# Edge lists on another queue, longer filling turns, and two normalisations tile by tile in a two-layer graph kernel

## The reference

```
xn = layernorm(x)
x  = x + relu(sum_i w[i] * (adj/degree)^i @ (xn @ W + b)) + gamma_norm(linear_attention(xn))
x  = x + top2_experts_16(layernorm(x))
xn = layernorm(x)
x  = x + gat(xn, edges) + linear_attention(xn) @ W_out + b_out
x  = x + top2_experts_8(layernorm(x))
```

## Time and profile before

| | |
|---|---|
| median of three runs | 230.09 us (229.31, 230.09, 230.31) |
| the profiled execution's own time | 230.77 us |
| its span | 229.1 us |
| mean granted TensorE clock | 0.968 |
| TensorE busy with matmuls | 215.6 us, 94% |
| VectorE busy | 138.9 us, 61% |
| ScalarE busy | 63.6 us, 28% |
| GpSimd busy | 21.2 us, 9% |
| chain that ended last | PE 88%, DVE 6%, DMA 2%, the rest 4% |

### The profile page before, as it was taken

How to read it: one execution, slowest core, us unless ns; L and a number is a source line. 1 busy time by engine, 2 the same in 40 slices (tenths; PEclk the granted TensorE clock), 3 DMA queues, 4 the chain that set the end, 5 groups by cost and what they waited for, 6 DMA issues and landing times.

```text
span 229.1 us, 2847 instructions
## 1 busy us (share of the span) xinstructions
PE 215.6 (94%) x989; PEld 142.1 (62%) x989; DVE 138.9 (61%) x414; ACT 63.6 (28%) x148; POOL 21.2 (9%) x36
## 2 busy tenths in 40 slices
PE   7399999998999799999999999999979999899994
PEld 4288455675589579854556686478754544758741
DVE  2799989958599442340636449797934764834202
ACT  2512755333220121110010149730643302013100
POOL 3680010000010200000050000000300010200000
PEclk9859999999999799999999999999999999999979
DMA  4899897599350000046040000000000000000002
GB/s 137 313 383 363 264 417 306 190 363 417 132 183 1 3 0 0 0 152 217 26 157 0 3 0 1 0 0 3 0 0 0 0 3 0 0 1 3 0 0 92
DMA packets 8669, 23.65 MB, mean 103 GB/s; under 512 B 2376, under 2 KB 2376, under 8 KB 8400
## 3 DMA queue, kind: packets, MB, share of 16 engines
q1 hardware_dynamic: 8656, 23.48, 28.3%
HBM read 22.95 MB, written 0.52 MB: 103 GB/s over the span
## 4 chain that ended last, share of the span: by engine, by line
PE 88%; DVE 6%; DMA 2%; issue 1%; POOL 1%; SPq 1%; ACT 0%; DVEq 0%
PE bank L1158 17%; PE bank L1132 13%; PE bank L1262 10%; PE bank L1250 10%; PE bank L1169 7%; PE bank L1207 6%; PE bank L1314 3%; PE bank L1213 3%; PE bank L1146 2%; PE bank L1214 2%; PE bank L1198 2%; DMA xa<-in_x 2%; DVE xT L604 2%; PE bank L1301 1%; PE bank L1351 1%
## 5 line engine op out<-in xcount | busy, mean ns | idle before, releaser
L1158 PE MATMUL bank<-raw,xT 128*128 128x512 f32 x88 | 39.2, 594 | 0.0
L1158 PEld LDWEIGHTS bank<-raw,xT 128*128 128x128 f32 x88 | 16.2, 190 | 18.3 <-issue 18.2
L309 POOL TENSOR_TENSOR rstd<-veps,minus_half 128x1 f32<-128x1 f32 x14 | 8.7, 632 | 163.0 <-DVE veps L591 89.0
L1262 PE MATMUL bank<-raw,ring 128*128 128x512 f32 x48 | 22.7, 634 | 0.0
L1250 PE MATMUL bank<-xT,raw 128*128 128x256 f32 x96 | 22.7, 386 | 0.0
L798 DVE TENSOR_SCALAR ring<-iota_bf,edges,radix 128x128 bf16<-128x128 bf16 x64 | 20.3, 359 | 0.0
L1250 PEld LDWEIGHTS bank<-xT,raw 128*128 128x128 f32 x96 | 17.6, 190 | 3.1 <-issue 0.9
L1301 PE MATMUL bank<-iota_bf 128*128 128x256 bf16 x121 | 17.6, 306 | 1.9 <-DVE iota_bf L775 1.6
L1169 PE MATMUL bank<-xT,raw 128*128 128x256 f32 x64 | 17.4, 434 | 0.8 <-DVE xT L604 0.8
L1262 PEld LDWEIGHTS bank<-raw,ring 128*128 128x128 f32 x48 | 9.6, 202 | 12.1 <-issue 11.7
L1301 PEld LDWEIGHTS bank<-iota_bf 128*128 128x128 bf16 x121 | 12.9, 108 | 5.8 <-DVE iota_bf L775 1.6
(11 more groups left out here) (256 smaller groups left out, 333.8 us busy)
## 6 DMA issues: line engine op xcount, KB each, us to landing
raw<-in_up SPq DMA_DIRECT2D x6, 512.0 KB, 8.6
raw<-in_down SPq DMA_DIRECT2D x6, 512.0 KB, 10.7
raw<-in_k SPq DMA_DIRECT2D x4, 512.0 KB, 9.7
raw<-in_q SPq DMA_DIRECT2D x4, 512.0 KB, 11.3
raw<-in_v SPq DMA_DIRECT2D x4, 512.0 KB, 9.8
raw<-in_out SPq DMA_DIRECT2D x4, 512.0 KB, 6.5
raw<-in_gat SPq DMA_DIRECT2D x4, 512.0 KB, 6.8
raw<-in_gnn SPq DMA_DIRECT2D x2, 512.0 KB, 10.7
```

The lines of the kernel that those rows point to most:

```text
L1158: ins = mm(bank[banks[t]][:, :], xT_at(c, t), w.at(c), start=c == 0, stop=c == C - 1)
L1262: ins = mm(dst, hid[:, m, cols], w.at(m), start=m == 0 and not opened, stop=m == k - 1)
```

## The change

Four edits:

- The two edge lists are issued by ScalarE, as the first two instructions of its block, and no longer by SyncE ahead of x.
- TensorE's idle turns before the first transposes are 30, not 20, and six more stand between those transposes and k0.
- In layer 0 the attention residual of a tile is complete in one piece (`mixture`): tile 0 ahead of diffusion step 0, tile 1 ahead of step 1. The third step's add, the residual, the statistics and the normalising pass run tile by tile (`residual`). TensorE transposes tile 0, runs the eight turns, and transposes tile 1.
- Before the last feed-forward the `elu`, the statistics and the normalising pass run tile by tile (`last_elu`). TensorE runs four turns, transposes tile 0, runs 24 turns, and transposes tile 1.

```diff
         def _(sp):
-            for a, n in enumerate(("src", "dst")):
-                sp.dma_start(edges_i[:, a, :], A[n].rearrange("(p j) -> p j", p=P)).then_inc(edges_in, 16)
             for t in range(T):
...
+            for a, n in enumerate(("src", "dst")):
+                nc.scalar.dma_start(edges_i[:, a, :], A[n].rearrange("(p j) -> p j", p=P)).then_inc(edges_in, 16)
             act.wait_ge(iota_bf_ready, 1)
             act.wait_ge(turn_ready, 1)
...
-            diffuse(0)
-
-            def centred(t):
+            def mixture(t):
+                dve.wait_ge(o_full, t + 1)
+                variance(1, t, bank[t][:, :])
                 go(V.scalar_tensor_tensor(mixed[:, t, :], bank[t][:, :], mv[:, t, 0:1], row["gamma0"],
                                           ALU.subtract, ALU.mult))
-
-            for t in range(T):
-                dve.wait_ge(o_full, t + 1)
-                variance(1, t, bank[t][:, :])
-                if t == 0:
-                    centred(0)
-            dve.wait_ge(step_read, 2)
-            diffuse(1)
-
-            centred(1)
-            settle()
-            for t in range(T):
+                settle()
                 dve.wait_ge(rstd_ready, T + t + 1)
                 V.scalar_tensor_tensor(mixed[:, t, :], mixed[:, t, :], rstd[:, t:t + 1], xa[:, t, :],
                                        ALU.mult, ALU.add).then_inc(mix_ready, 1)
+
+            mixture(0)
+            diffuse(0)
+            mixture(1)
+            dve.wait_ge(step_read, 2)
+            diffuse(1)
             dve.wait_ge(step_read, 4)
             dve.wait_ge(mix_ready, 2)
 
-            for t in range(T):
-                add_step(2, t)
-            for t in range(T):
+            def residual(t):
                 dve.wait_ge(step_read, 4 + t + 1)
                 go(V.scalar_tensor_tensor(xb[:, t, :], diffused[:, t, :], 0.0, mixed[:, t, :], ALU.max, ALU.add))
-            variances(2, lambda t: xb[:, t, :])
+                settle()
+                variance(2, t, xb[:, t, :])
+
+            add_step(2, 0)
+            residual(0)
+            add_step(2, 1)
             dve.wait_ge(xT_full, 2)
-            for t in range(T):
-                norm_rows(2, xn[:, t, :], xb[:, t, :], t)
+            norm_rows(2, xn[:, 0, :], xb[:, 0, :], 0)
+            residual(1)
+            norm_rows(2, xn[:, 1, :], xb[:, 1, :], 1)
...
-            elu(1, xb, summed, mixed, go)
-            variances(6, lambda t: xb[:, t, :])
-            for t in range(T):
+            def last_elu(t):
+                dve.wait_ge(y_ready, T + t + 1)
+                go(V.scalar_tensor_tensor(mixed[:, t, :], g_a[:, t, :], 0.0, summed(t), ALU.max, ALU.add))
+                settle()
+                dve.wait_ge(elu_exp, T + t + 1)
+                go(V.scalar_tensor_tensor(xb[:, t, :], g_b[:, t, :], 1.0, mixed[:, t, :], ALU.min, ALU.add))
+                settle()
+                variance(6, t, xb[:, t, :])
+
+            for t in range(T):
+                last_elu(t)
                 norm_rows(6, xn[:, t, :], xb[:, t, :], t)
...
-            idle_turns(1, 20)
+            idle_turns(1, 30)
             pe.wait_ge(consts, 1)
             xT_made(0, xn, (0, 1))
+            idle_turns(2, 6)
             k_of("k0", k_full, 0)
...
+            xT_made(1, xn, (4, 5), (0,))
             idle_turns(5, 8)
-            xT_made(1, xn, (4, 5))
+            xT_made(1, xn, (4, 5), (1,))
...
-            idle_turns(4, 40)
-            xT_made(4, xn, (3, 4))
+            idle_turns(4, 4)
+            xT_made(4, xn, (3, 4), (0,))
+            idle_turns(4, 24)
+            xT_made(4, xn, (3, 4), (1,))
```

## The result

The changed kernel took 233.60 us (median of four runs, 232.48 to 233.77) beside 229.70 us of the kernel before (229.15 to 230.31): ratio 1.0173 [1.0129, 1.0217] (in brackets the 95% interval), slower, where 226.5 was predicted. Both deny the prediction. Both kernels spread over almost 5 us from run to run, and the changed one's time goes with its mean granted clock: 228.5 to 228.9 at 0.975 to 0.977, 230.2 to 230.6 at 0.968 or 0.969, 233.4 and 233.5 at 0.953 and 0.955. The first four runs all lay at the dear end (233.61 at 0.956 in the profiled one), where only four of the twelve later ones lie; whether four in a row were chance stays open.

The account below looks back on a forecast made before the run. The prediction took TensorE's own time and the few places where it waits as the bound. Terms -3.0 + 0.7 - 1.6 = -3.9 gave 226.9 or 226.2, stated as 226.5 us; range 225.6 to 227.5, widened to 224.6 to 229.0.

Parts of the forecast that it names:

- Part 1, -3.0: Start: x issued earlier and more idle turns keep the clock up beside k0; last counts end near 38.55, -3.0 us.
- 6.9 predicted: Start: k0's records at the upper clock level take 6.9 us, not 9.93.
- 0.8 or less: Start: TensorE idles 0.8 us or less before the normalised rows come, instead of 2.70.
- the one-hots are late next: Start: first counts wait for VectorE's one-hots and end at 19.6 instead of 23.00, a gain of 3.4 us.
- The 0.8 for an earlier x: Start: x, issued 0.91 us earlier, lands 0.8 us sooner.
- I had allowed them 0.6 us: Start: edges landing up to 0.6 us later still hide behind an x that lands at 4.9.
- Rival 4: Start: late edges delay the statistics; total +2.9, 233.4 us; slower once edges land after 5.8; chance 0.04.
- Part 2, +0.7: Middle of layer 0: TensorE waits 0.7 us for low parts before the third diffusion step; +0.7 us.
- nothing is gained and the 0.7 stays: Middle of layer 0: VectorE is ready for both halves in time, TensorE's work stays the same; the 0.7 us wait remains.
- rival 3: Middle of layer 0: the clock falls earlier, while narrow records still run; term +2.3, total 228.1 us; chance 0.14.
- The rule that I set against this row: Middle of layer 0: clock follows recent busyness, so no fall behind 5 us of unbroken work; sum 1.6 us lower.
- Part 3, -1.6: Before the last feed-forward: tile 0's work runs in VectorE's wait, tile 1 ends at 198.35 instead of 199.98; -1.6 us.

Follow-up runs that it names:

- the larger comparison: The changed kernel repeated without an edit (12 runs) beside more runs of the kernel before (30), on one chip: 230.33 against 230.55 us, ratio 0.9988.
- the part alone: Kernel before with only the start changed: edges on ScalarE's queue, 30 and 6 idle turns; 230.95 us, ratio 1.0011.
- part 2 alone: Kernel before with only the middle of layer 0 changed, in VectorE's order and TensorE's turns; 231.58 us, ratio 1.0088.
- the wide products: Narrow attention-weight products made 128 columns wide by repeating columns; on the changed kernel 226.41 us, with the middle of layer 0 in the old order 226.22.
- the change without part 2: Changed kernel with the middle of layer 0 as before, start and last feed-forward edits kept; 228.91 us, ratio 0.9822.
- the kernel with the lowest median: Kernel before with products 128 columns wide, the tile-by-tile last feed-forward, and 30 and 6 idle turns, edges still on SyncE; 224.03 us, ratio 0.9777.

## Why the prediction was wrong

**Part 1, -3.0: half right, and read from one unlucky start.** The kinds held: k0 at a granted clock of 1.00 takes 7.14 us (6.9 predicted), though TensorE stood for 1.68 us before the transposes and not for 0.8 or less, the one-hots are late next (TensorE's loads wait for VectorE's ring at 20.05), and the last counts end 2.1 us earlier. Two sizes failed. The 0.8 for an earlier x was 0.36 (5.84 to 5.48), because the statistics now wait for the edges, converted at 4.62 instead of 3.37. I had allowed them 0.6 us; they took 1.25. Rival 4 named this wait, with its point of decision at a landing of 5.8, which they did not reach. And the profiled start of before was no typical one: x was late there (5.84) and k0 took 9.93. In four other traces with the edges and x issued as before, x is there at 5.05 to 5.20; in one, at 6.07. Out0 then begins at 53.59 to 53.70 with the old turns, against 54.85 in the profiled execution of before. With part 1 it begins at 52.58 to 52.91. So the part is worth about 0.9 us there, not 3.0, and by the part alone (1.0011) even that is lost further on. In the larger comparison this term is the furthest off.

**Part 2, +0.7: the step that failed in the first comparison.** The forecast of the wait was right, in place and nearly in size (0.47 us before the third step, forecast 0.7), and VectorE had both tiles ready (71.15 and 74.10) before TensorE asked. What failed is "nothing is gained and the 0.7 stays", that is, a clock that falls only behind the narrow records. In the first profile the part took 6.6 us: from 2.1 early to 4.5 late. Of these 0.5 are the wait, 1.1 the diffusion step (65.69 to 68.83 for 2.08), 4.8 the narrow records, 0.3 the rest. That is rival 3's mechanism, priced there at "as much again" as 1.7; a whole narrow stretch at half rate costs 4.8. I had its price in the rows: 48 records at twice 0.11 us. Over ten runs part 2 alone costs 1.1 us by the medians and 2.0 by the ratio, and with the wide products no cost shows. So the price is that of the clock and not of the order, as far as these runs tell: the fall came at 66.5 and 71.3 us in two traces of the same kernel, and kernels without part 2 have low stretches of up to 14 us as well.

The rule that I set against this row says that the clock follows how busy the engine has been (the Trainium skill, TensorE: Matmul & The Clock Gate, What's actually happening). If busy is what the profile shows as busy, the traces disagree for narrow records: TensorE ran without a gap from 65.69 to 78.88, and the granted clock was 0.50 from 67 on. The same section of the Trainium skill says that what watches the activity runs free of the kernel's start, so that the moment of the change behind the first matmuls shifts by half a microsecond either way. The traces agree that changes shift from run to run, and for this fall, in the middle of a kernel, by more: 66.5 and 71.3 us in the same kernel, whose 48 records took 10.05 and 6.62 us.

**Part 3, -1.6: right.** The delay shrinks from 4.5 to 2.8 us between layer 0 and the router, so -1.7; tile 1 is normalised by 202.81, 3.9 us after out1's end at 198.9 (forecast 3.8). Alone it gave 0.9909, -2.1 us (-1.2 by the medians of all runs).

**The sum.** Forecast were -3.0, +0.7 and -1.6; the parts alone gave +0.3, +2.0 and -2.1 by the ratios, and the whole -0.3 [-1.3, +0.8]. Two steps failed: that the clock of the middle falls only behind the narrow records, which cost 6.6 us in the first trace, and that the start of one trace is the kernel's, which made -3.0 out of -0.9. Two of the signs named for being wrong came: the statistics waited for the edges, and the middle lost more than 1 us. The range reached from 224.6 to 229.0 because it took the clock's place in one trace for the kernel's. The three times shown of before already lay 1.0 us apart, by which I corrected the level (0.7) but no term. The sums of three rivals are 0.1 to 0.2 off (0.7 and 1.7 make 2.4 for rival 3, not 2.3); nothing hangs on that.

## What to carry over

A stretch of very narrow matmuls can cost twice its time in some runs and not in others. Where a record's time doesn't depend on its columns, repeat the columns: on the kernel before that alone gave 0.9927 [0.9892, 0.9962] and took away two thirds of the spread, on the changed kernel it gained 3.9 us and left the spread as wide (224.49 to 229.74), and with part 3 and the longer filling the kernel runs at 0.9777 [0.9723, 0.9831]. Before an edit is priced from one trace, ask which of its stretches lie at the lower clock, and look at several executions: a term that hangs on them is a spread, not a number.

## What the runs showed of the hardware

- **Narrow work and the clock.** Records of 2 and 16 columns brought the clock down while TensorE was busy without a gap (0.50 from 67 us on in the changed kernel, from 75 in the kernel before); the same number at 128 columns, in the same time, did not (1.00 in seven traces).
- **The granted clock column can read 1.00 while records run slowly.** With the old filling, six records of k0 stand in 12 to 14 us and ten in 14 to 16 (windows above), all at 1.00, and the transposes ahead of them took 1.94 us instead of 1.18. TensorE had idled for 2.4 us. The length of that idling does not decide it alone: with the longer filling the transposes took 1.18 us and k0 7.14 behind 1.90 us of it (the change without part 2), with the old one 1.94 and 8.82 behind 1.78 (the kernel before with wide products). What held them is open.
- **Edges issued beside x landed later.** On ScalarE's queue beside x `dst` took 3.4 us (3.3 to 3.6 in seven traces) instead of 1.9 (1.9 to 2.1 ahead of x on SyncE's):

```profile
far<-in_dst ACTq DMA_DIRECT2D x1, 32.0 KB, 3.4
```

  The Trainium skill (DMA: Bandwidth & Descriptors, Issuing engines are not separate DMA queues) says that transfers of several engines interleave on the same 16 DMA engines and that only issue time is saved. The rows agree on the saving: x was issued 0.91 us earlier. They show a loss beside it, 1.5 us of landing; whether the other queue or x beside them made it was not tried.
- **GpSimd's fillings held VectorE** (1.35 and 2.00 us for 0.23 and 0.19). The Trainium skill (SBUF — State Buffer, SBUF: two separate sides) says that the two share a pair of ports by an exclusive lock, for some of VectorE's instructions; the rows agree, as these two end within 0.1 us of the fillings.
- **The last 16 products** have a low stretch of their own in ten of the fourteen traces, and its length changes: they take 8.8 us before and after, 10.0 in the repeat of the changed kernel and in the changed kernel with wide products, and 7.1 without one in the trace of the kernel with the lowest median. What decides it wasn't tried.
